# Layer 2 of a graph network: the last 72 of 196 steps of a strand gather a key and two projections in one row, and the picked projection is stored in edge order

## The chip, the cores and the metric

The kernel runs on one core of one Trainium2 chip. The metric is the device time of one execution in microseconds. A core has TensorE (matrix products, "PE"), VectorE ("DVE"), ScalarE ("ACT"), GpSimd ("POOL") and SyncE ("SP"); each runs its own instructions in order, and they wait for each other through semaphores. Plain DMAs are issued here by SP and ScalarE; the gathers, whose row numbers come from data, are issued by GpSimd. All share 16 DMA engines.

## The reference

Four graph layers run over 6250 nodes with 128 features and 100000 edges, each edge with a source, a target and one of 32 types. The change is in the third layer (layer 2):

```python
q = (x @ Wq_w + Wq_b)[dst]
k_base = (x @ Wk1)[src] + (h_rel @ Wk2)[edge_type] + Wk_b
score_base = jnp.sum(q * k_base, axis=-1)
scores = (score_base[:, None] + q @ v_rule.T) * scale
...                                   # softmax over edges of one target and one type, mean over 4 rules: attn_mean
proj = jnp.einsum('nd,rdo->nro', x, W_r)        # 32 projections of every node
msg = proj[src, edge_type] * attn_mean[:, None]
out = jax.ops.segment_sum(msg, dst, num_segments=n_nodes) + bias
```

So an edge needs two rows that hang on its source: the key x @ Wk1 of the source, for the score, and the projection of the source by the edge's type, for the message.

## The kernel before

Edges are sorted by target and lie in 128 partitions of 784; each partition's 784 edges are four strands of 196 steps (`STRANDS`, `STRIDE`). Nodes lie 50 to a partition (`NB`).

The score stage of layer 2 is `scores_and_projections` (names `l2s_...`). It goes through 98 turns of two steps, eight columns of 128 edges each. In each turn GpSimd issues eight gathers (line 2686), each fetching a 512-byte key for one edge per partition from `table_k` into one of six slots of `krow` (`KRING`). SP loads the rows with the queries, spread by target, into one of two slots of `zrow` (line 2695). VectorE carries the query along the strand, multiplies it with the keys and reduces (lines 2616 to 2631). GpSimd may fill a slot again when VectorE has used it. In 22 late turns one of the eight columns isn't gathered: TensorE picks it out of the keys in SBUF with one-hot matrices that VectorE and ScalarE write (`LatePicks`, lines 2515 to 2562).

Beside this, and independent of it, TensorE multiplies each of the 50 blocks of 128 nodes with the 32 weight matrices (line 2644). ScalarE copies the products into one of two halves of `proj` (line 2658) and stores it into the table `g.proj` in device memory (line 2662), 100 stores of 128 x 8 KB.

Then comes the sum of layer 2, `sum_strands` (names `l2z_...`), with the attention in front of it: VectorE makes the row numbers (lines 2384 and 2385), then the softmax (lines 2395 to 2461). Meanwhile GpSimd begins to gather the projections from `g.proj`, 784 gathers of 128 rows of 512 bytes (line 1104), 16 to a turn, into one of six slots (`RING`). In a turn VectorE weighs 16 columns (lines 1137, 1138) and then adds step by step over four strands (lines 1069, 1070); SP stores the running sums of each step in `g.prefix` (line 1113). The last turn of 16 is cut in two.

`tail2` (names `l2y_...`) begins by joining the four strands of each partition and the partitions among each other (`StrandCompletion`: four gathers at line 1300, a scan over 512 numbers, four scatters at line 1304); then GpSimd fetches the sum of every node (line 1376).

## Time and profile before

| what | us |
|---|---|
| three timed runs, median (lowest to highest) | 6673.84 (6673.53 to 6675.8) |
| the profiled execution | 6672.9 |
| its span in the trace | 6671.0 |

Shares of the span: VectorE 76%, GpSimd 69%, TensorE 50%, ScalarE 15%. The chain of waits that ended last covers only the last 1% of the span here, so it doesn't tell which stage is bound by what; the windows and the groups by line do. In the rows below, times are microseconds from the start of the span unless marked ns. A gather's row on GpSimd is the time in which it writes the transfer's descriptors, not the transfer. The queue q10 carries the DMAs that ScalarE issues, q1 those of SP and q0 those of GpSimd; a queue's share is the time of its packets, summed and divided by 16 engines and the window.

### The profile page before, as it was taken

The page shows a single profiled execution, that of the slowest core. Times are in us where ns is not written, and L with a number is a line of the kernel's source. Part 1 is how long each engine was busy: PE and PEld are TensorE (multiplying, and loading weights), DVE is VectorE, ACT ScalarE, POOL GpSimd, SP SyncE. Part 2 cuts the span into 40 slices and gives each one's busy share as a digit, 9 for nine tenths or more (in the row PEclk, how much of TensorE's full clock was granted, in tenths as well). Part 3 has the DMA queues.
Part 4 walks back from the last instruction along what each step waited for, and adds up shares of the span by engine and source line. Part 5 has one row for each costly group of instructions (what it writes and reads, how often), then busy time and mean ns, then how long its engine had stood idle before and what let it go on. Part 6 is the DMA issues. An engine that isn't in the chain of part 4 may idle for free. (4 is left out here: it accounts for less than half of the span.)

```text
span 6671.0 us, 61345 instructions
## 1 busy us (share of the span) xinstructions
PE 3327.2 (50%) x21638; PEld 2955.3 (44%) x21638; DVE 5039.4 (76%) x7174; ACT 998.4 (15%) x2297; POOL 4601.4 (69%) x4753
## 2 busy tenths in 40 slices
PE   7530117467777457777468847730000004777770
PEld 5530106367777457777443327730000003777770
DVE  8999998678898677787647779986443446888886
ACT  1013333200000010000034435520000003000002
POOL 0027777777777677777667777777777767777774
PEclk9999558789988778888789978865555556888885
DMA  3036020134444344444339974433343332333332
GB/s 60 1 149 255 2 36 13 26 86 115 114 115 115 99 115 109 110 110 110 99 131 345 354 264 126 122 87 107 103 109 103 104 91 59 112 112 112 112 112 71
DMA packets 588107, 763.09 MB, mean 114 GB/s; under 512 B 118267, under 2 KB 479585, under 8 KB 568345
## 3 DMA queue, kind: packets, MB, share of 16 engines
q1 hardware_dynamic: 416916, 375.57, 17.6%
q0 software_dynamic: 152672, 272.57, 17.2%
q10 hardware_dynamic: 18210, 111.02, 4.3%
q8 instruction: 171, 2.80, 0.2%
q14 instruction: 138, 1.13, 0.1%
HBM read 346.63 MB, written 412.16 MB: 114 GB/s over the span
## 5 line engine op out<-in xcount | busy, mean ns | idle before, releaser
L1104 POOL DMA_INDIRECT l2z_rows<-proj,l2z_idx x784 | 765.6, 977 | 246.1 <-issue 238.6
L2686 POOL DMA_INDIRECT l2s_krow<-table_k,l2s_idx x762 | 720.9, 946 | 232.3 <-issue 231.3
L1104 POOL DMA_INDIRECT l0z_rows<-table,l0z_idx x736 | 697.2, 947 | 234.7 <-issue 224.0
L928 POOL DMA_INDIRECT l3z_rows<-table,l3z_idx x736 | 694.4, 944 | 234.7 <-issue 224.0
L1104 POOL DMA_INDIRECT l1z_rows<-table,l1z_idx x736 | 694.5, 944 | 233.3 <-issue 214.0
L837 PE MATMUL l3z_pfound<-l3h_hn,l3h_hot 128*128 128x130 f32 x4800 | 642.4, 303 | 236.3 <-DVE l3h_hot L814 236.3
L837 PE MATMUL l1z_pfound<-g_x,l2o_xT 128*128 128x128 f32 x4800 | 638.3, 303 | 238.9 <-DVE l2o_xT L814 238.9
L837 PEld LDWEIGHTS l3z_pfound<-l3h_hn,l3h_hot 128*128 128x128 f32 x4800 | 634.5, 218 | 244.2 <-issue 237.2
L837 PEld LDWEIGHTS l1z_pfound<-g_x,l2o_xT 128*128 128x128 f32 x4800 | 630.5, 218 | 246.6 <-issue 239.0
L2098 POOL DMA_INDIRECT first_sj<-scores,first_atdst x504 | 525.8, 1043 | 169.5 <-issue 169.5
L837 PE MATMUL l0z_pfound<-first_rows,l0r_hot 128*128 128x140 f32 x3648 | 475.3, 294 | 91.5 <-DVE l0r_hot L814 91.5
L837 PEld LDWEIGHTS l0z_pfound<-first_rows,l0r_hot 128*128 128x128 f32 x3648 | 465.3, 200 | 102.1 <-DVE l0r_hot L814 102.1
L1137 DVE TENSOR_TENSOR l2z_msg<-l2z_rows,l2z_factors 128x1024 f32<-128x1024 f32 (+1 forms) x50 | 60.0, 1200 | 512.6 <-DMA l2z_rows<-proj,l2z_idx 512.2
L2644 PE MATMUL l2s_bank<-l2o_wr,l2o_xT 128*128 128x512 f32 x800 | 373.0, 622 | 93.8 <-ACT l2s_proj L2658 76.4
L814 DVE TENSOR_TENSOR l2o_xT<-l1z_pcode,l1z_pnames 128x3200 f32<-128x3200 f32 x96 | 330.2, 3481 | 21.8 <-PE l1z_pcode L823 21.7
L814 DVE TENSOR_TENSOR l3h_hot<-l3z_pcode,l3z_pnames 128x3200 f32<-128x3200 f32 x96 | 330.3, 3482 | 11.9 <-PE l3z_pcode L823 11.5
L607 POOL IOTA sd_nidi<- 128x50 int32 x1 | 0.2, 170 | 429.0 <-POOLq L60 429.0
L2542 PE MATMUL l2s_bank<-l2o_kn,l2o_xT 128*128 128x128 f32 x2200 | 291.4, 302 | 5.3 <-DVE l2o_xT L2523 5.3
L2542 PEld LDWEIGHTS l2s_bank<-l2o_kn,l2o_xT 128*128 128x128 f32 x2200 | 290.8, 219 | 5.4 <-issue 5.4
L2644 PEld LDWEIGHTS l2s_bank<-l2o_wr,l2o_xT 128*128 128x128 f32 x800 | 154.3, 198 | 312.2 <-issue 171.2
L900 DVE SCALAR_TENSOR_TENSOR l3z_acc<-l3z_acc,l3z_xx,l3z_msg 128x128 f32<-128x128 f32 x784 | 271.7, 347 | 25.9
L268 PE MATMUL sd_turn<-g_ident,prep_key 128*128 128x128 f32 x112 | 27.6, 428 | 487.3 <-DVE prep_key L245 481.8
(619 smaller groups left out, 7595.9 us busy)
## 6 DMA issues: line engine op xcount, KB each, us to landing
proj<-l2s_proj ACTq DMA_DIRECT2D x100, 1024.0 KB
spread_q<-prep_zero SPq DMA_DIRECT2D x98, 656.0 KB
l2s_zrow<-spread_q SPq DMA_DIRECT2D x98, 656.0 KB
prefix<-l0z_acc SPq DMA_DIRECT2D x196, 256.0 KB
prefix<-l2o_kn SPq DMA_DIRECT2D x196, 256.0 KB
prefix<-l2z_acc SPq DMA_DIRECT2D x196, 256.0 KB
prefix<-l3z_acc SPq DMA_DIRECT2D x48, 1040.0 KB
l2z_rows<-proj,l2z_idx POOLq DMA_INDIRECT x784
```

What stands on the lines that cost most here:

```text
L268: mm = self.nc.tensor.transpose(self.turn[q][:, u], self.keys[at % 2][:, c:c + P], self.g.ident[:])
L607: nc.gpsimd.iota(nid_i[:], pattern=[[1, NB]], base=EP, channel_multiplier=NB).then_inc(numbered, 1)
L814: self.nc.vector.tensor_tensor(self.hot[i][:, 0:hi - lo], bc_mid(self.code[:], hi - lo), bc_last(self.names[:, lo:hi], P), ALU.is_equal).t ...
L837: mm = self.nc.tensor.matmul(self.found[:], self.hot[i][:, b - lo], self.nodes[:, b], start=b == 0, stop=b == NB - 1)
L900: v.scalar_tensor_tensor(acc[:, c, u, 0:D], sum_before(k, u)[:, 0:D], w.factor(k, lo, u), msg[:, u], ALU.mult, ALU.add).then_inc(summed, 1)
L928: nc.gpsimd.indirect_dma_start(out=rows[:, k % RING, u, :], out_offset=None, in_=table, in_offset=bass.IndirectOffsetOnAxis(ap=idx[:, lo + ...
L1104: nc.gpsimd.indirect_dma_start(out=rows[:, k % RING, c * (hi - lo) + u, :], out_offset=None, in_=table, in_offset=bass.IndirectOffsetOnAxi ...
L1137: chain.add(self.v.tensor_tensor(msg[:, 0:half], rows[:, 0:half], bc_last3(factor[:, 0:half], D), ALU.mult))
L2098: nc.gpsimd.indirect_dma_start(out=sj[:, j, :], out_offset=None, in_=g.scores0, in_offset=bass.IndirectOffsetOnAxis(ap=at_dst[:, j:j + 1], ...
L2542: mm = self.nc.tensor.matmul(self.found, self.hot[:, b], self.nodes[:, b], start=b == 0, stop=b == NB - 1)
L2644: mm = nc.tensor.matmul(bank[m % 2][:, b], xT[:, i, :], wr[:, c:c + wide], start=True, stop=True)
L2686: nc.gpsimd.indirect_dma_start(out=krow[:, k % KRING, c * (hi - lo) + u, :], out_offset=None, in_=g.table_k, in_offset=bass.IndirectOffset ...
```

## The change

The last 72 of each strand's 196 steps ("late") are treated otherwise than the first 124 ("early").

- The projection table gets one and a half times as many rows: for each node and each pair of types three rows stand side by side, the even type's projection, the node's key, and the odd type's projection. ScalarE copies the key between them, one copy more per half block, and the 100 stores are 128 x 12 KB each.
- In the score stage the early part (62 turns) is as before, without `LatePicks`: all 496 keys are gathered. When all stores of the table have landed, GpSimd gathers in the late part (36 turns, 288 gathers) rows of 1536 bytes, key and two projections, into four places that lie over the room of `krow` and `proj`. VectorE uses the key in the middle. ScalarE scales the identity matrix by 1 or 0 for each column and parity; TensorE multiplies both projections with these and adds, so that the one of the edge's type is left; ScalarE copies it and stores it in edge order into `g.late`.
- The sum (`sum_halves`) treats the early and late steps as separate strands, eight in a partition, in turns of 16 columns: 31 early ones, gathered by GpSimd into four slots, and 18 late ones between them, loaded from `g.late` by SP in plain DMAs of 1 MB into two slots. Each part has one accumulator instead of two in turn. The last turn isn't cut.
- VectorE computes ends for eight half strands at the start of the score stage (`HalfEnds`), and the completion joins eight (`HalfCompletion`): eight gathers and scatters, a scan over 1024 numbers. The row numbers of the projections take six operations more.

```diff
+EARLY_STEPS, LATE_STEPS = 124, STRIDE - 124
+HALVES = 2 * STRANDS
+SLOTS = TYPES // 2 * 3
+EARLY, LATE = 4, 2
+PARTS = [(0, EARLY_STEPS), (EARLY_STEPS, STRIDE)]
+def both_parts():
+    n = [(hi - lo) // ABREAST for lo, hi in PARTS]
+    order = []
+    for i in range(n[0]):
+        order += [(1, m) for m in range(n[1] * i // n[0], n[1] * (i + 1) // n[0])] + [(0, i)]
+    return [(h, i, PARTS[h][0] + i * ABREAST, PARTS[h][0] + (i + 1) * ABREAST) for h, i in order]
...
+    def on_vector(self, chain):
+        v, g, keep, run, own = self.nc.vector, self.g, self.order.keep[:], self.run, self.base
+        lead = self.halves.full[:]
+        for s in range(HALVES):
+            lo, hi = (s // 2 * STRIDE + at for at in PARTS[s % 2])
+            chain.add(v.memset(run[:, lo:lo + 1], float(lo)))
+            chain.add(v.tensor_tensor_scan(run[:, lo + 1:hi], keep[:, lo + 1:hi], keep[:, lo + 1:hi], 1.0, ALU.mult, ALU.min))
+            chain.add(v.tensor_scalar(own[:, s:s + 1], g.part[:], float(HALVES), float(EP + 1 + s), ALU.mult, ALU.add))
...
+        chain(v.tensor_copy(self.halves.at_i[:], lead))
+        for h, (lo, hi) in enumerate(PARTS):
+            chain.add(v.tensor_reduce(self.halves.full[:, h::2], strands(keep, lo, hi), AX, ALU.min))
...
+class HalfCompletion:
...
+    def on_pool(self, pool):
+        where = self.halves.at_i
+        for s in range(HALVES):
+            self.nc.gpsimd.indirect_dma_start(out=self.row[:, s, :], out_offset=None, in_=self.prefix,
+                                              in_offset=bass.IndirectOffsetOnAxis(ap=where[:, s:s + 1], axis=0)).then_inc(self.lead, 16)
+        for s in range(HALVES):
+            pool.wait_ge(self.fixed, s + 1)
+            self.nc.gpsimd.indirect_dma_start(out=self.prefix, out_offset=bass.IndirectOffsetOnAxis(ap=where[:, s:s + 1], axis=0),
+                                              in_=self.row[:, s, :], in_offset=None).then_inc(self.sent, 16)
+        pool.wait_ge(self.sent, 16 * HALVES)
...
+        eng.wait_ge(self.turned, 1)
+        v.tensor_copy(self.tail[:], self.ps.rearrange("p (s q) -> p q s", s=HALVES)).then_inc(self.cleared, 1)
...
+        v.tensor_tensor_scan(shifted[:, 1:n], full[:, 0:n - 1], tail[:, 0:n - 1], 0.0, ALU.mult, ALU.add).then_inc(self.moved, 1)
+        eng.wait_ge(self.lead, 16 * HALVES)
+        eng.wait_ge(self.returned, 1)
+        for s in range(HALVES):
+            at = s // 2 * STRIDE + PARTS[s % 2][0]
+            v.scalar_tensor_tensor(self.row[:, s], self.back[:, s], self.order.keep[:, at:at + 1], self.row[:, s],
+                                   ALU.mult, ALU.add).then_inc(self.fixed, 1)
+def sum_halves(nc, name, g, order, table, late, prefix, halves, weight, aside):
+    with Space(nc, name) as s:
+        rows = s.sb("rows", [P, EARLY + LATE, WIDTH, D])
+        msg = s.sb("msg", [P, WIDTH, D])
+        acc = s.sb("acc", [P, 2, WIDTH, D])
...
+                for k, (h, i, lo, hi) in enumerate(turns):
+                    aside.on_vector(eng, chain, k)
+                    if k == 0:
+                        chain(v.tensor_copy(factors[:], by_step(weight)))
+                    if h:
+                        eng.wait_ge(got_late[i % LATE], 16 * (i // LATE + 1))
+                    else:
+                        eng.wait_ge(got_early[i % EARLY], 16 * n * (i // EARLY + 1))
+                    if i:
+                        eng.wait_ge(stored[h], 16 * ABREAST * i)
...
+                v.tensor_copy(g.tail[:], last[0])
+                v.tensor_copy(halves.tails[:], last[1])
...
+                for i, k in enumerate(early_turns):
+                    lo, hi = turns[k][2:]
+                    if i >= EARLY:
+                        hold(pool, weighed, early_turns[i - EARLY] + 1)
+                    for u in range(hi - lo):
+                        for c in range(STRANDS):
+                            nc.gpsimd.indirect_dma_start(out=rows[:, slot(i, 0), c * (hi - lo) + u, :], out_offset=None, in_=table,
+                                                         in_offset=bass.IndirectOffsetOnAxis(ap=idx[:, c, lo + u:lo + u + 1], axis=0)).then_inc(got_early[i % EARLY], 16)
...
+                def fetch(i):
+                    lo, hi = (at - EARLY_STEPS for at in turns[late_turns[i]][2:])
+                    sp.dma_start(rows[:, slot(i, 1), 0:STRANDS * (hi - lo)].rearrange("p (c u) f -> p c (u f)", c=STRANDS),
+                                 ready[:, :, lo * D:hi * D]).then_inc(got_late[i % LATE], 16)
+                for i in range(LATE):
+                    fetch(i)
+                done = 0
+                for k, (h, i, lo, hi) in enumerate(turns):
+                    for u in range(hi - lo):
+                        done += 1
+                        sp.wait_ge(summed, done)
+                        sp.dma_start(out[:, :, (lo + u) * D:(lo + u + 1) * D], by_strand(acc[:, h, 0:STRANDS * (hi - lo)])[:, :, u]).then_inc(stored[h], 16)
+                    if h and i + LATE < len(late_turns):
+                        sp.wait_ge(weighed, k + 1)
+                        fetch(i + LATE)
...
-        chain(v.scalar_tensor_tensor(self.most[:], g.src[:, 0:NC], float(TYPES), g.type[:], ALU.mult, ALU.add))
-        return v.tensor_copy(idx[:], self.most[:])
+        most, odd, bits = self.most, self.lead, self.trail[:].bitcast(I32)
+        chain(v.tensor_copy(bits, g.type[:]))
+        chain(v.tensor_scalar(bits, bits, 1, None, ALU.bitwise_and))
+        chain(v.tensor_copy(odd[:], bits))
+        chain(v.scalar_tensor_tensor(most[:], g.type[:], 3.0, odd[:], ALU.mult, ALU.add))
+        chain(v.tensor_scalar(most[:], most[:], 0.5, None, ALU.mult))
+        chain(v.scalar_tensor_tensor(most[:], g.src[:, 0:NC], float(SLOTS), most[:], ALU.mult, ALU.add))
+        return v.tensor_copy(idx[:], strands(most[:], 0, EARLY_STEPS))
...
-class LatePicks:
...
+        room = s.sb("room", [P, PLACES * n * place])
+        krow = room[:, 0:KRING * n * D].rearrange("p (r x f) -> p r x f", r=KRING, x=n)
+        proj = room[:, KRING * n * D:].rearrange("p (h j y f) -> p h j y f", h=2, j=TYPES // 4, y=3)
+        triple = room[:].rearrange("p (r x f) -> p r x f", r=PLACES, x=n)
...
-        late = range(54, len(turns), 2)
-        picks = LatePicks(nc, s, g, kn, xT, [(STRANDS - 1) * STRIDE + turns[k][1] - 1 for k in late], [bank[0][:, c, 0:P] for c in range(2)], bank[1][:, 0, 0:P])
...
-                picks.start(chain)
+                v.tensor_copy(strands(idx[:], 0, EARLY_STEPS), strands(g.src[:, 0:NC], 0, EARLY_STEPS)).then_inc(indexed, 1)
+                bits, odd, where = qv[:, 1].bitcast(I32), qv[:, 2], qv[:, 3]
...
+                ends.on_vector(chain)
...
+                    if m < 0:
+                        eng.wait_ge(got[k % KRING], 16 * n * (k // KRING + 1))
+                        keys = krow[:, k % KRING]
+                    else:
+                        eng.wait_ge(taken[at(m)], 16 * n * (m // PLACES + 1))
+                        keys = triple[:, at(m), :, D:2 * D]
+                    chain(v.tensor_tensor(prod[:, 0:n], keys, qrow[:, :, 0:D], ALU.mult))
...
-                picks.on_tensor(pe)
+                for m in range(len(turns) - early):
+                    pe.wait_ge(marked, m + 1)
+                    pe.wait_ge(taken[at(m)], 16 * n * (m // PLACES + 1))
+                    if m >= 2:
+                        pe.wait_ge(moved, m - 1)
+                    out = bank[m % 2][:].rearrange("p b (x f) -> p (b x) f", f=D)
+                    for x in range(n):
+                        for y in range(2):
+                            mm = nc.tensor.matmul(out[:, x], marks[:, m % 2, x, y], triple[:, at(m), x, 2 * y * D:(2 * y + 1) * D],
+                                                  start=y == 0, stop=y == 1)
+                    mm.then_inc(chosen, 1)
...
+                            c.copy(proj[:, h, :, 1], kn[:, i].unsqueeze(1).to_broadcast([P, TYPES // 4, D])).then_inc(between, 1)
...
+                        c.copy(proj[:, h, j:j + 4, 0::2], bank[m % 2][:].rearrange("p b (j y f) -> p (b j) y f", y=2, f=D)).then_inc(copied, 1)
...
+                            act.dma_start(table[:, i, h * SLOTS // 2 * D:(h + 1) * SLOTS // 2 * D],
+                                          proj[:, h].rearrange("p j y f -> p (j y f)")).then_inc(stored[h], 16)
...
+                def mark(m):
+                    if m >= 2:
+                        act.wait_ge(chosen, m - 1)
+                    for x in range(n):
+                        for y in range(2):
+                            made = c.activation(marks[:, m % 2, x, y], g.ident[:], ACT.Copy, scale=choice[:, y, x // 2, 2 * m + x % 2:2 * m + x % 2 + 1])
+                    made.then_inc(marked, 1)
+                last = len(turns) - early
+                mark(0)
+                for m in range(last):
+                    if m + 1 < last:
+                        mark(m + 1)
+                    act.wait_ge(chosen, m + 1)
+                    if m >= 2:
+                        act.wait_ge(sent[m % 2], 16 * (m // 2))
+                    c.copy(chosen_rows[:, m % 2], bank[m % 2][:].rearrange("p b (x f) -> p (b x) f", f=D)).then_inc(moved, 1)
+                    act.wait_ge(moved, m + 1)
+                    act.dma_start(ready[:, :, 2 * m * D:(2 * m + 2) * D],
+                                  chosen_rows[:, m % 2].rearrange("p (c u) f -> p c (u f)", c=STRANDS)).then_inc(sent[m % 2], 16)
...
+                pool.wait_ge(stored[0], 16 * NB)
+                pool.wait_ge(stored[1], 16 * NB)
+                both = g.proj.rearrange("(n r) f -> n (r f)", r=3)
+                for m, (lo, hi) in enumerate(turns[early:]):
+                    if m >= PLACES:
+                        pool.wait_ge(chosen, m - PLACES + 1)
+                        hold(pool, used, early + m - PLACES + 1)
+                    elif m >= 2:
+                        hold(pool, used, early)
+                    for u in range(hi - lo):
+                        for c in range(STRANDS):
+                            j = c * STRIDE + lo + u
+                            nc.gpsimd.indirect_dma_start(out=triple[:, at(m), c * (hi - lo) + u, :], out_offset=None, in_=both,
+                                                         in_offset=bass.IndirectOffsetOnAxis(ap=idx[:, j:j + 1], axis=0)).then_inc(taken[at(m)], 16)
...
-                sum_strands(nc, "l2z", g, O.dst, g.proj, g.prefix, D, Weighed(attn[:]), Beside(attention, tab3))
+                sum_halves(nc, "l2z", g, O.dst, g.proj, g.late, g.prefix, halves, attn[:], Beside(attention, tab3))
```

## Rows read from the trace of the kernel before

**Rows 1.** The page, costliest groups: line, operation, count | busy us, mean ns | idle before.

```profile
L1104 POOL DMA_INDIRECT l2z_rows<-proj,l2z_idx x784 | 765.6, 977 | 246.1 <-issue 238.6
```

**Rows 2.** Windows of GpSimd's gathers in the sum: window, length, busy (count), clock, DMA.

```profile
4445.20:4541.60 96.40, 79.24 (x57) 0.50 0.16 41
...
4541.60:5450.00 908.40, 686.37 (x728) 0.50 0.40 109
```

**Rows 3.** Window of all engines: PE, PEld, DVE, ACT, POOL, clock, DMA share, GB/s.

```profile
4540.00:5454.00 914.00, 0.58 (x2) 0.50 (x2) 385.27 (x493) 0.00 (x0) 687.67 (x729) 0.50 0.40 108
```

**Rows 4.** Gathers by tile: shortest/median/longest ns, first and last start (512-, 16-byte rows).

```profile
L2686 POOL DMA_INDIRECT l2s_krow<-table_k,l2s_idx x762: 940/944/1193, 3485.0 to 4436.9; - x191
...
L2098 POOL DMA_INDIRECT first_sj<-scores,first_atdst x504: 940/944/2149, 440.3 to 1206.6; - x168
```

**Rows 5.** Timeline of VectorE, the start of two following score turns.

```profile
4405.54 0.85 DVE L2616 TENSOR_TENSOR l2s_qrow<-l2s_qrow,g_dokeep 128x656 f32<-128x656 f32 x1
...
4413.68 0.85 DVE L2616 TENSOR_TENSOR l2s_qrow<-l2s_qrow,g_dokeep 128x656 f32<-128x656 f32 x1
```

**Rows 6.** Line 2662, the stores of the projections: issue ns, first and last issue.

```profile
L2662 ACTq DMA_DIRECT2D proj<-l2s_proj x100: 326/326/341, 3485.7 to 3932.5; - x100
```

**Rows 7.** Window of all engines over those stores, columns as in the third group.

```profile
3485.70:3937.00 451.30, 367.31 (x794) 151.95 (x792) 318.82 (x488) 199.90 (x212) 341.26 (x362) 0.96 0.95 351
```

**Rows 8.** DMA queues from 3500 to 3550 us: packets, MB, share of 16 engines.

```profile
q10 hardware_dynamic: 1460, 10.64, 51.1%
q1 hardware_dynamic: 2624, 3.34, 23.6%
q0 software_dynamic: 1280, 2.62, 17.8%
```

**Rows 9.** Groups by line, whole span: count | busy us, mean ns | idle before.

```profile
L2644 PE MATMUL l2s_bank<-l2o_wr,l2o_xT 128*128 128x512 f32 x800 | 373.0, 622 | 93.8 <-ACT l2s_proj L2658 76.4 <-PEq L60 14.7 <-issue 2.7
L2542 PE MATMUL l2s_bank<-l2o_kn,l2o_xT 128*128 128x128 f32 x2200 | 291.4, 302 | 5.3 <-DVE l2o_xT L2523 5.3
L2658 ACT COPY l2s_proj<-l2s_bank 128x1024 f32<-128x1024 f32 x200 | 198.3, 1013 | 268.9 <-DMA proj<-l2s_proj 145.4 <-PE l2s_bank L2644 123.2
L2555 ACT ACTIVATE l2o_xT<-l2s_bank,l2s_pnames 128x128 f32<-128x128 f32 x572 | 151.8, 401 | 234.6 <-PE l2s_bank L2542 233.7 <-PE l2s_bank L2528 0.9
```

**Rows 10.** DMA issues: count, KB each, median us from issue to landing.

```profile
table_q<-l1y_qn SPq DMA_DIRECT2D x12, 328.0 KB, 2.8
```

**Rows 11.** DMA queues from 4800 to 4850 us (512-byte rows out, projections in).

```profile
q0 software_dynamic: 1287, 2.65, 21.7%
q1 hardware_dynamic: 5280, 2.62, 17.9%
```

**Rows 12.** DMA queues from 1000 to 1050 us, gathers of 16-byte rows.

```profile
q0 software_dynamic: 1062, 0.07, 5.3%
```

**Rows 13.** Timeline of the attention and of a turn of the sum.

```profile
4468.29 4.17 POOL L1104 DMA_INDIRECT l2z_rows<-proj,l2z_idx  x1 [0.30 <-issue]
...
4539.05 1.22 DVE L1137 TENSOR_TENSOR l2z_msg<-l2z_rows,l2z_factors 128x1024 f32<-128x1024 f32 x1
...
4547.40 1.22 DVE L1137 TENSOR_TENSOR l2z_msg<-l2z_rows,l2z_factors 128x1024 f32<-128x1024 f32 x1
```

**Rows 14.** Timeline of the ends of both stages and of the completion.

```profile
4436.86 0.95 POOL L2686 DMA_INDIRECT l2s_krow<-table_k,l2s_idx  x1 [0.30 <-issue]
...
4443.45 0.97 DVE L2384 SCALAR_TENSOR_TENSOR l_attn<-g_src,g_type 128x784 f32<-128x784 f32 x1 [1.13 <-PEq L60]
...
5448.60 0.95 POOL L1104 DMA_INDIRECT l2z_rows<-proj,l2z_idx  x1 [0.31 <-issue]
...
5451.07 0.69 DVE L1137 TENSOR_TENSOR l2z_msg<-l2z_rows,l2z_factors 128x512 f32<-128x512 f32 x1 [5.20 <-DMA l2z_rows<-proj,l2z_idx]
...
5460.85 0.94 POOL L1300 DMA_INDIRECT l2y_leadrow<-prefix,g_dostrandi  x1 [11.30 <-POOLq L60]
...
5474.07 0.98 POOL L1376 DMA_INDIRECT l2y_agg<-prefix,g_doendi  x1 [1.54 <-DMA prefix<-l2y_leadrow,g_dostrandi]
```

More of the change, by code:

```diff
@@ new lines, with __init__ @@
+class HalfEnds:
+    def __init__(self, nc, g, order, halves, run, base):
+        self.nc, self.g, self.order, self.halves, self.run, self.base = nc, g, order, halves, run, base
+    def on_vector(self, chain):
[6 more added lines that the diff above has]
+            chain.add(v.tensor_scalar(own[:, s:s + 1], g.part[:], float(HALVES), float(EP + 1 + s), ALU.mult, ALU.add))
+        chain.until()
+        for h, (lo, hi) in enumerate(PARTS):
+            chain.add(v.tensor_reduce(lead[:, h::2], strands(run, lo, hi), AX, ALU.add))
+        chain.until()
+        chain(v.scalar_tensor_tensor(lead, g.part[:].to_broadcast([P, HALVES]), float(NC), lead, ALU.mult, ALU.add))
+        chain(v.tensor_tensor(lead, lead, own, ALU.subtract))
+        for h, (lo, hi) in enumerate(PARTS):
+            chain.add(v.tensor_tensor(lead[:, h::2], lead[:, h::2], strands(keep, lo, lo + 1)[:, :, 0], ALU.mult))
+        chain.until()
+        chain(v.tensor_tensor(lead, lead, own, ALU.add))
+        chain(v.tensor_copy(self.halves.at_i[:], lead))
+        for h, (lo, hi) in enumerate(PARTS):
+            chain.add(v.tensor_reduce(self.halves.full[:, h::2], strands(keep, lo, hi), AX, ALU.min))
+        chain.until()
@@ L1732, in tail2 @@
         xT = s.sb("xT", [P, 2, GROUP, P])
-        tp, ph = s.ps("tp", [P, GROUP, P]), [s.ps(f"ph{u}", [P, W3]) for u in range(GROUP)]
-        done = StrandCompletion(nc, s, g, O.dst, g.prefix, tp[:], s.ps("cpb", [P, STRANDS, P])[:])
+        turns_ps, ph = s.ps("tp", [P, HALVES * P]), [s.ps(f"ph{u}", [P, W3]) for u in range(GROUP)]
+        tp = turns_ps[:, 0:GROUP * P].rearrange("p (u q) -> p u q", u=GROUP)
+        done = HalfCompletion(nc, s, g, O.dst, halves, g.prefix, turns_ps[:], s.ps("cpb", [P, HALVES, P])[:])
         inner, outer = Norm(nc, s, g, "a"), Norm(nc, s, g, "b")
@@ L2586, in scores_and_projections, with at @@
         stepped, used = s.sem("stepped"), s.sem("used")
-        multiplied, copied = s.sem("multiplied"), s.sem("copied")
+        multiplied, copied, between = s.sem("multiplied"), s.sem("copied"), s.sem("between")
+        marked, chosen, moved = s.sem("marked"), s.sem("chosen"), s.sem("moved")
         stored = [s.sem(f"stored{h}") for h in range(2)]
-        late = range(54, len(turns), 2)
-        picks = LatePicks(nc, s, g, kn, xT, [(STRANDS - 1) * STRIDE + turns[k][1] - 1 for k in late], [bank[0][:, c, 0:P] for c in range(2)], bank[1][:, 0, 0:P])
-        def landed(k):
-            return 16 * sum(n - (m in late) for m in range(k % KRING, k + 1, KRING))
+        sent = [s.sem(f"sent{h}") for h in range(2)]
         got, zgot = [s.sem(f"got{r}") for r in range(KRING)], [s.sem(f"zgot{h}") for h in range(2)]
+        taken = [s.sem(f"taken{r}") for r in range(PLACES)]
+        ends = HalfEnds(nc, g, order, halves, qv[:, 0], own[:])
+        def at(m):
+            return (m + 2) % PLACES
         with s.block() as block:
@@ L2649, in _ @@
             @block.scalar
             def _(act):
[L2651 removed]
+                c = nc.scalar
+                table = g.proj.rearrange("(p b r) f -> p b (r f)", b=NB, r=SLOTS)
                 for i in range(NB):
                     for k in range(pairs):
[L2654 to L2656 removed]
+                        m, h, j = i * pairs + k, k // 2, k % 2 * 4
+                        if k % 2 == 0:
+                            if i:
+                                act.wait_ge(stored[h], 16 * i)
+                            c.copy(proj[:, h, :, 1], kn[:, i].unsqueeze(1).to_broadcast([P, TYPES // 4, D])).then_inc(between, 1)
@@ L2657, in _ @@
                         act.wait_ge(multiplied, m + 1)
-                        nc.scalar.copy(proj[:, c], bank[m % 2][:].rearrange("p b f -> p (b f)")).then_inc(copied, 1)
+                        c.copy(proj[:, h, j:j + 4, 0::2], bank[m % 2][:].rearrange("p b (j y f) -> p (b j) y f", y=2, f=D)).then_inc(copied, 1)
                         if k % 2:
                             act.wait_ge(copied, m + 1)
-                            c = slice(2 * (k - 1) * wide, 2 * (k + 1) * wide)
-                            act.dma_start(table[:, i, c], proj[:, c]).then_inc(stored[h], 16)
@@ L2663, in _ @@
-                picks.squares(act, 0)
-                for m, k in enumerate(late):
-                    picks.squares(act, m + 1)
-                    act.wait_ge(used, k - KRING + 1)
-                    picks.place(act, m, krow[:, k % KRING, n - 1])
+                            act.wait_ge(between, 2 * i + h + 1)
+                            act.dma_start(table[:, i, h * SLOTS // 2 * D:(h + 1) * SLOTS // 2 * D],
+                                          proj[:, h].rearrange("p j y f -> p (j y f)")).then_inc(stored[h], 16)
@@ L2677, in _ @@
                 pool.wait_ge(indexed, 1)
-                for k, (lo, hi) in enumerate(turns):
+                for k in range(early):
+                    lo, hi = turns[k]
                     if k >= KRING:
```

196 lines of the change are left out of this document (120 added, 76 removed).

## The prediction

> **What bounds the kernel now.** I read the costliest groups of the page first: at their head stand the 784 gathers that GpSimd issues in the sum of layer 2 [rows 1]; the windows then say how densely. In the sum, after its attention, 728 gathers fill 908.4 us, so one is issued every 908.4/728 = 1.248 us [rows 2]; there VectorE is busy 385 of 914 us and the DMA engines 0.40 of the time, at a granted TensorE clock of 0.50 with PE idle [rows 3]. In the score stage the first and the last of 762 gathers start 951.9 us apart, 1.251 us each [rows 4]. A VectorE turn there takes 8.14 us with its wait in it [rows 5], eight gathers 9.98 us. So both stages last as long as GpSimd needs to issue their gathers; what takes a gather away from GpSimd takes 1.248 us from the kernel, until something else is late. The exception is a stretch at the start of the score stage: from 3485.7 to 3937 us the DMA engines are 0.95 busy while the projections are stored [rows 6, 7]; GpSimd is not slowed by it yet, because nothing in that stage waits for the stores.
>
> All sums are made against the profiled execution, 6672.9 us; the median of the timed runs is 6673.84, 0.9 us more, which is below what I can resolve.
>
> **Part 1: gathers removed and added.** The sum gathers 31 turns x 16 = 496 rows instead of 784: 288 x 1.248 = **-359.4 us**. All 288 lie behind the attention, where no VectorE work stretches them: in the attention's 96.4 us only 57 gathers are issued [rows 2], and the new ring of four slots of 16 has room for 64, so the smaller ring costs nothing there. The score stage gathers 784 again instead of 762 (the 22 rows that TensorE picked are gone): 22 x 1.25 = **+27.5 us**. The one-hot work that goes with those picks (VectorE, ScalarE, TensorE) was beside GpSimd's issue and gives nothing back.
>
> Is a gather of 1536 bytes a row issued as fast as one of 512? The trace has none. Gathers of 16-byte rows take 944 ns (median), gathers of 512-byte rows 944 ns [rows 4]: no dependence on bytes over a factor of 32. I take 1.248 us; the other bound, three times that price, is the last rival.
>
> **Part 2: GpSimd now waits for the projection stores.** The first wide gather may start only when all 100 stores have landed. They grow from 104.9 MB (100 x 128 x 8 KB) to 157.3 MB. Before, the stores ran from 3485.7 us until about 3937 [rows 6]: 104.9/451 = 0.2325 MB/us. The upper bound on that rate comes from the queues' shares: keys and spread rows take 17.8% + 23.6%, leaving 58.5%, and the store queue moves 10.64 MB in 50 us at 51.1%, or 0.416 MB/us alone [rows 8]; 0.585 x 0.416 = 0.243 MB/us. GpSimd's early part is 496 x 1.2485 = 619 us, from 3485 to 4104, plus 3 us for the longer VectorE start (below): 4107. By then 144 MB are stored (150 at the upper rate); 13 MB remain (7). With the other two queues silent the rate rises, limited by two buffers: filling one takes three copies of about 1.01 us [rows 9] and the issue, 3.4 us, landing 2.8 (a store of 328 KB [rows 10]), moving 1.57 MB at 0.416 3.8 us; half of 10.0 is 5.0 us for 1.57 MB, 0.315 MB/us. 13/0.315 = **+41 us** of wait; between 15 (upper rate, all through) and 60 (a rate of 0.223). What hides the third copy per buffer is that ScalarE waits for landed stores 145 us in this stage [rows 9]. TensorE needs 373/50 = 7.5 us of a block's 13 us [rows 9].
>
> **Part 3: what the 36 late turns contain.** A turn is 8 wide gathers, 9.98 us of GpSimd. Beside it: VectorE 7.4 to 8.1 us as before [rows 5]. TensorE: 16 products, two instructions each, at 291.4/2200 = 0.132 us [rows 9], 4.2 us; twice that, 8.5, at the clock of 0.50 that [rows 3] shows. ScalarE: 16 scaled identities at 151.8/572 = 0.265 (throughput) to 0.401 us (one alone) [rows 9], 4.2 to 6.4 us, a copy of 1.01 and an issue: 5.6 to 7.8 us. Marks and banks are double-buffered, so these run side by side; each is below 9.98. DMA time per engine: 32 packets of spread rows at 0.236 x 800 us/2624 = 72 ns, 2.3 us [rows 8]; 32 kilobyte packets of the store between 46 and 54 ns (a 512-byte one takes 27.1 ns [rows 11]), 1.5 to 1.7 us; 64 wide rows. A 512-byte row of the projection table takes 0.217 x 800/1287/4 = 33.7 ns, a 16-byte row 0.053 x 800/1062/4 = 10 ns [rows 11, 12]; the line through both gives 82 ns for 1536 bytes, the bounds are 59 (at the store queue's 0.416 MB/us) and 101 (three times 33.7): 3.8 to 6.5 us. Sum 9.1 us, between 7.6 and 10.5, against 9.98. That is close. I take **0** for excess, because the mid value fits and a share of 0.95 was reached in [rows 7]; the upper end, 10.5/0.95 = 11.05, would cost 36 x 1.07 = +38.
>
> **Part 4: edges.** (a) Score stage's start: some 35 small VectorE operations more, about 14 us by their sizes. VectorE then starts 7 us later, which six turns of ring hide, but it slows GpSimd's issue: in the attention's 96.4 us, 57 gathers went out where 77 fit [rows 2], a quarter lost; of 14 us **+3** (0 to 5). The Trainium skill, page "SBUF — State Buffer", section "Who interferes with whom", says that a VectorE instruction with two SBUF inputs or in a two-port mode shuts GpSimd out for its whole length; by it only the new scans and two-input operations would count, an estimate of 3 us or less. The trace agrees in the one place where they meet: a gather takes 4.17 us beside such an operation [rows 13]. (b) Score stage's end: from the last gather's end (4437.8) to the next stage's first work (4443.45) were 5.7 us [rows 14]. Now the last turn goes landing 1.5 [rows 14], TensorE 4.2 to 8.5, copy 1.0, issue 0.4, landing of the store 2.8 [rows 10], block end 1: about 14.5, **+9** (5 to 14). (c) Indices: six more VectorE operations before GpSimd may start, **+3.2**. (d) The sum's last turn is 16 rows instead of 8, with 8.35 us of VectorE [rows 13] instead of some 4, and a second copy of tails: **+4.5**. (e) The completion joins 8 half strands instead of 4: four gathers and four scatters more in the 13.2 us from 5460.85 to 5474.07 [rows 14], 8 x 1.27 = 10.2; its longer chain of transposes and copies lies beside the lead gathers: **+10.5** (6 to 15).
>
> (f) VectorE in the sum: 49 turns x 8.35 = 409 us plus 99 for the attention, and 12 places where two early turns follow each other and the second waits some 3 us for the first one's stores: 545 us after the stage's start. GpSimd ends at 5 + 96 + 439 x 1.248 = 649. So GpSimd stays the bound with 100 us to spare. SP now also issues 18 loads of 1 MB in order among its stores; a slot has three turns until it is needed.
>
> **Sum.** -359.4 + 27.5 + 41 + 3 + 9 + 3.2 + 4.5 + 10.5 = -260.7; 6672.9 - 260.7 = **6412 us**. With the low ends of the bounds (wait 15, start 0, tail 5, completion 6) 6374; with the high ends but no excess of the late turns 6442; with it 6480.
>
> **Rivals.** (1) *Transfers bound the late turns*: 11.05 us a turn, 6412 + 38 = 6450. For it: 9.1 of 9.98 is near the limit, and three queues meet. Against: the shares of [rows 8] leave room, and the rings hold four turns. The Trainium skill, page "DMA: Bandwidth & Descriptors", section "Measured", gives 0.95 us for a transfer of 64 KB and 6.15 for 1 MB; a line between them makes 1.6 us for 192 KB, an estimate of 13.1 us a turn and 6526 us. The row says otherwise: a 64 KB gather takes 0.217 x 50/41 = 0.26 us of the engines' time [rows 11], since neighbours overlap, so that figure is no end of my range.
>
> (2) *Picking is serial*: marks, products and copy of one turn follow each other, 6.4 + 8.5 + 1.3 = 16.2 us a turn, 36 x 6.2 = +224: 6636. For it: ScalarE does both marks and copies in one order. Against: marks of the next turn are issued before the wait for this turn's products.
>
> (3) *VectorE becomes the sum's bound*: with one accumulator per part, every turn waits for a store behind a 1 MB load, 8.35 + 5.8 us x 49 + 99 = 792 instead of 649: +143, 6555. Against: the parts alternate in 36 of 48 steps.
>
> (4) *Slower than before*: GpSimd's price of a wide gather grows with its bytes. Place: the issue of the 288 late gathers. At three times 1.248 it is +719: 7131. It decides from 261/288 = 0.91 us more a gather, an issue every 2.16 us. Against it: 944 ns at 16 and at 512 bytes [rows 4]; for it only that no row is wider than 656 bytes.
>
> **How the numbers follow.** Forecast 0.72, rival 1 0.12, rival 2 0.07, rival 3 0.04, rival 4 0.05. The range 6374 to 6480 takes in the forecast's bounds and rival 1; rivals 2 to 4 (0.16) and a little of the rest are outside. Everything but rival 4 is faster: 0.94 faster, 0.05 slower, 0.01 within 0.2%, which is about what a measurement of this kernel can tell from no change.
>
> **What would show it.** The sum's gathers 1.248 us apart and the stage some 650 us to its last one; a gap of GpSimd near 4107 us that ends with the last projection store near 4148; the late gathers about 944 ns each and 9.98 us a turn. Rival 1 shows as GpSimd waiting in the late turns with a DMA share over 0.95; rival 2 as VectorE done and GpSimd waiting for TensorE; rival 3 as VectorE waiting for prefix stores; rival 4 as longer gathers. A gap much over 60 us would make part 2 wrong, a turn over 11 us part 3.

## The result, and the profile after

The changed kernel takes **6370.4 us** (median; 6368.2 to 6373.4), the kernel before 6673.7: a ratio of 0.9545 [0.9529, 0.9562]. The profiled execution took 6371.9, its span 6370.0, 301.0 less than before. The forecast was 6412 with a range from 6374: right in direction, 42 us too slow, and 3.6 us outside at the low end.

The gathers by tile (operation, count: shortest/median/longest ns, first and last start) answer to [rows 4]; below them is what GpSimd waited for ahead of its wide gathers (us, times):

```profile
L2896 POOL DMA_INDIRECT l2s_room<-table_k,l2s_idx x496: 940/944/1194, 3485.6 to 4105.7; - x166
L2911 POOL DMA_INDIRECT l2s_room<-proj,l2s_idx x288: 942/946/1164, 4106.9 to 4466.5; - x144
...
  issue: 85.9, 282
  DVE l_base L2809: 1.8, 6
```

A wide gather (line 2911) is issued in 946 ns, a key gather in 944. GpSimd lost 1.8 us to VectorE in the late turns, nothing to TensorE, and nothing to the stores. GpSimd's timeline at the four seams of layer 2, with what ended its wait in brackets:

```profile
4105.70 0.94 POOL L2896 DMA_INDIRECT l2s_room<-table_k,l2s_idx  x1 [0.30 <-issue]
4106.95 0.95 POOL L2911 DMA_INDIRECT l2s_room<-proj,l2s_idx  x1 [0.30 <-issue]
...
4466.54 0.94 POOL L2911 DMA_INDIRECT l2s_room<-proj,l2s_idx  x1 [0.30 <-issue]
4488.48 0.94 POOL L1304 DMA_INDIRECT l2z_rows<-proj,l2z_idx  x1 [20.99 <-DVE l2z_idx L2606]
...
5131.90 0.94 POOL L1304 DMA_INDIRECT l2z_rows<-proj,l2z_idx  x1 [0.30 <-issue]
...
5172.76 0.98 POOL L1590 DMA_INDIRECT l2y_agg<-prefix,g_doendi  x1 [1.53 <-DMA prefix<-l2y_leadrow,l_ati]
```

Between the last key gather and the first wide one lie the usual 0.30 us: the wait for the stores, put at 41 us, is not there. The stores (line 2853, answering to [rows 6]) show why:

```profile
L2853 ACTq DMA_DIRECT2D proj<-l2s_room x100: 326/326/350, 3485.8 to 4069.1; - x100
```

The last was issued at 4069.1. In the three runs below in which GpSimd does wait for it, the wait ends 5.9 to 8.5 us after that issue; so all had landed by about 4077 here, some 30 us before GpSimd asked. The forecast had them end near 4148.

The windows of the late turns and of the sum (PE, PEld, DVE, ACT, POOL busy, clock, DMA share, GB/s) answer to [rows 3, 7], the group of the sum's gathers to [rows 1]:

```profile
4146.00:4466.00 320.00, 158.55 (x1024) 153.38 (x1024) 228.71 (x351) 184.74 (x545) 242.33 (x256) 0.75 0.86 275
...
4488.00:5132.00 644.00, 6.84 (x27) 4.09 (x27) 470.62 (x549) 3.43 (x4) 492.69 (x496) 0.50 0.54 156
```

```profile
L1304 POOL DMA_INDIRECT l2z_rows<-proj,l2z_idx x496 | 493.5, 995 | 171.8 <-issue 148.7
```

In late turns no engine is full and the DMA engines are 0.86 busy: GpSimd's issue still sets the pace, as it does in the sum. Where the 301 us came from, by first and last gathers:

| stretch | before | after | difference | forecast |
|---|---|---|---|---|
| start of the span to the first key gather | 3485.0 | 3485.6 | +0.6 | +3 |
| first to last gather of the score stage | 951.9 | 980.9 | +29.0 | +27.5 and 41 of wait |
| on to the first gather of the sum | 8.4 | 21.9 | +13.5 | +12.2 |
| first to last gather of the sum | 1003.3 | 643.4 | -359.9 | -359.4 |
| on to the first gather of node sums | 25.5 | 40.9 | +15.4 | +15.0 |

The five differences add up to -301.4, the span fell by 301.0. Every term but one fits within 3 us, and the sum without the wait, 6412 - 41 = 6371, is the profiled time to 1 us. That last agreement is partly luck: the other terms are off by -2.4, +1.5, +1.3, -0.5 and +0.4, which cancel.

### The profile page after: what moved, and what is told of

Same layout as the page of the kernel before. It is cut to its first block and busy times, and to the rows that moved or that the text cites. A ratio compares the mean times of both kernels' runs of the same rounds, so it can differ in the third digit from the quotient of the medians.

```text
span 6370.0 us, 58942 instructions
## 1 busy us (share of the span) xinstructions
PE 3257.2 (51%) x20526; PEld 2848.6 (45%) x20526; DVE 4990.7 (78%) x7203; ACT 1071.1 (17%) x2371; POOL 4365.4 (69%) x4495
## 5 line engine op out<-in xcount | busy, mean ns | idle before, releaser
L1304 POOL DMA_INDIRECT l2z_rows<-proj,l2z_idx x496 | 493.5, 995 | 171.8 <-issue 148.7
L2896 POOL DMA_INDIRECT l2s_room<-table_k,l2s_idx x496 | 470.2, 948 | 151.1 <-issue 151.1
L2822 PE MATMUL l2s_bank<-l2o_wr,l2o_xT 128*128 128x512 f32 x800 | 417.6, 675 | 184.8 <-ACT l2s_room L2849 170.1
L2911 POOL DMA_INDIRECT l2s_room<-proj,l2s_idx x288 | 273.1, 948 | 87.7 <-issue 85.9
L2806 DVE TENSOR_TENSOR l2s_prod<-l2s_room,l2s_qrow 128x1024 f32<-128x1024 f32 x98 | 119.5, 1220 | 254.4 <-DMA l2s_room<-table_k,l2s_idx 160.3
L2833 PE MATMUL l2s_bank<-l2s_room,l2o_xT 128*128 128x128 f32 x1152 | 184.1, 335 | 226.3 <-issue 153.2
L2833 PEld LDWEIGHTS l2s_bank<-l2s_room,l2o_xT 128*128 128x128 f32 x1152 | 178.3, 248 | 232.7 <-issue 216.2
```

The lines of the kernel that those rows point to most:

```text
L1304: nc.gpsimd.indirect_dma_start(out=rows[:, slot(i, 0), c * (hi - lo) + u, :], out_offset=None, in_=table, in_offset=bass.IndirectOffsetOnA ...
L2806: chain(v.tensor_tensor(prod[:, 0:n], keys, qrow[:, :, 0:D], ALU.mult))
L2822: mm = nc.tensor.matmul(bank[m % 2][:, b], xT[:, i, :], wr[:, c:c + wide], start=True, stop=True)
L2833: mm = nc.tensor.matmul(out[:, x], marks[:, m % 2, x, y], triple[:, at(m), x, 2 * y * D:(2 * y + 1) * D], start=y == 0, stop=y == 1)
L2896: nc.gpsimd.indirect_dma_start(out=krow[:, k % KRING, c * (hi - lo) + u, :], out_offset=None, in_=g.table_k, in_offset=bass.IndirectOffset ...
L2911: nc.gpsimd.indirect_dma_start(out=triple[:, at(m), c * (hi - lo) + u, :], out_offset=None, in_=both, in_offset=bass.IndirectOffsetOnAxis( ...
```

## Why the stores were early: the queues

The DMA queues over 400 us in the thick of the stores (packets, MB, share of 16 engines; q10 the stores, q1 the spread rows, q0 the gathers). Before:

```profile
q10 hardware_dynamic: 12620, 91.85, 56.5%
q1 hardware_dynamic: 20644, 26.27, 21.3%
q0 software_dynamic: 10236, 20.99, 16.9%
```

After:

```profile
q10 hardware_dynamic: 9628, 105.14, 63.7%
q1 hardware_dynamic: 21073, 26.81, 20.7%
q0 software_dynamic: 10224, 20.95, 15.2%
```

The forecast left 58.5% for the stores, since the other two queues held 41.4% [rows 8]. They did not hold it. For the same bytes (47.3 and 47.8 MB) they show 38.2% over these 400 us before and 35.9% after, and the stores take 63.7%. The store queue moved 0.263 MB/us instead of 0.230. What differs is how often ScalarE had nothing to send: with a buffer free it waited 96.6 us for products before, and 16.5 us after. Its waits over the same 400 us (us in total, times, longest), before and then after:

```profile
ACT l2s_proj L2658 <- DMA proj<-l2s_proj: 131.2, 46, 5.5
ACT l2s_proj L2658 <- PE l2s_bank L2644: 96.6, 91, 3.0
```

```profile
ACT l2s_room L2847 <- DMA proj<-l2s_room: 188.2, 67, 5.5
ACT l2s_room L2849 <- PE l2s_bank L2822: 16.5, 18, 2.0
```

Before, ScalarE waited in turn for a buffer and for TensorE, which itself waits for ScalarE's copies [rows 9]; while one half is filled, only the other can be on its way. With stores of 1.5 times the bytes that gap comes once per 1.57 MB instead of 1.05, and the products are ready when a buffer is. That is **theory A**: the rate of before was set by its two buffers, not by the engines. **Theory B**: longer rows (12 KB instead of 8) move at a better price. The forecast's own reading was a third: the other queues' shares are a fixed price and the engines were as good as full.

## Experiments

**Before, with three store buffers of 8 KB instead of two.** The bytes and row lengths are those of before, so B and the fixed shares expect no change of the store rate.

```diff
-        proj = s.sb("proj", [P, TYPES * D])
+        proj = s.sb("proj", [P, 3, 4 * wide])
...
-        stored = [s.sem(f"stored{h}") for h in range(2)]
+        stored = [s.sem(f"stored{h}") for h in range(3)]
...
+                        h = at % 3
+                        if at >= 3 and k % 2 == 0:
+                            act.wait_ge(stored[h], 16 * (at // 3))
```

> The kernel before with three store buffers of 8 KB a partition in place of two, nothing else. Theory A (before the change the store queue ran dry between stores, because a buffer was filled only after its last store had landed): the stores keep the queue full, move 0.26 to 0.27 MB/us as after the change, the last is issued near 3875 us in place of 3932.5, the DMA share of the stretch rises from 0.95 to about 1.0. Theory B (rows of 12 KB are cheaper per byte than rows of 8 KB): the rate stays near 0.233 MB/us and the last store is issued between 3920 and 3935. Time by both: 6674 us, no change, since nothing waits for the stores.

The time did not move: 6673.7 against 6673.6, ratio 1.000 [0.9989, 1.0010]; nobody waits for these stores. But they were issued until 3845.4 instead of 3932.5 [rows 6]. First the line of the stores, then the queues from 3500 to 3840 us:

```profile
L2663 ACTq DMA_DIRECT2D proj<-l2s_proj x100: 325/326/341, 3488.1 to 3845.4; - x100
```

```profile
q10 hardware_dynamic: 13541, 98.61, 69.2%
q1 hardware_dynamic: 17409, 22.15, 18.6%
q0 software_dynamic: 8674, 17.79, 13.9%
```

The stores moved 98.61/340 = 0.290 MB/us, a fifth over the "upper bound" of 0.243; the small queues fell to 32.5% at an unchanged 0.117 MB/us (39.94/340; before 47.26/400 = 0.118). Theory A holds in direction, and a queue's share is no fixed price. Its figures were too low: it expected 0.26 to 0.27 MB/us and a last issue near 3875, because it took the queue of the change as full. The change's two buffers leave gaps too. [rows 7] with its 351 GB/s and share of 0.95 was a queue that ran dry, not a limit.

TensorE's clock is another rival: a faster TensorE would leave shorter gaps as well. The windows of the kernel before, of the change (both 3500 to 3900 us) and of the three buffers (3500 to 3840) show busy times, granted clock, DMA share and GB/s:

```profile
3500.00:3900.00 400.00, 326.53 (x700) 135.32 (x701) 289.17 (x443) 174.40 (x176) 302.50 (x320) 0.96 0.95 348
...
3500.00:3900.00 400.00, 280.84 (x536) 110.49 (x536) 288.15 (x440) 195.10 (x202) 302.66 (x320) 0.90 1.00 383
...
3500.00:3840.00 340.00, 329.38 (x754) 140.09 (x752) 244.06 (x372) 188.29 (x189) 257.40 (x272) 1.00 1.02 408
```

The change stores faster than the kernel before at a lower mean clock, 0.90 against 0.96, so the clock isn't the reason there. With three buffers it is 1.00, the higher of its two levels (2.4 GHz) throughout, where the other means mix it with the lower one; TensorE waited only 10.0 us for ScalarE's copies there, before 71.0 in its 400 us. But 4% more clock doesn't make 26% more stores. Each rate comes from one profile, and rates vary: in the run without picked keys below, which leaves the store loop as it is, two 8 KB buffers moved 86.60 MB in the same 400 us, 0.217 MB/us, at a clock of 0.91. That is 6% less than before; the differences read here are 14% and 26%.

**The change, each store sent as two of 6 KB rows**, same buffers: theory B expects a slower rate, theory A the same.

```diff
-                                act.wait_ge(stored[h], 16 * i)
+                                act.wait_ge(stored[h], 32 * i)
...
-                            act.dma_start(table[:, i, h * SLOTS // 2 * D:(h + 1) * SLOTS // 2 * D],
-                                          proj[:, h].rearrange("p j y f -> p (j y f)")).then_inc(stored[h], 16)
+                            for part in range(2):
+                                lo, size = h * SLOTS // 2 * D + part * SLOTS // 4 * D, SLOTS // 4 * D
+                                act.dma_start(table[:, i, lo:lo + size],
+                                              proj[:, h, 4 * part:4 * part + 4].rearrange("p j y f -> p (j y f)")).then_inc(stored[h], 16)
```

> The changed kernel with each store of 128 x 12 KB issued as two DMAs of 128 x 6 KB, one behind the other, same bytes and same waits. Theory A (queue kept full): the last store is issued within 10 us of 4069 and the time stays at 6370 us. Theory B (long rows): at 6 KB the keys' and spread rows' queues take 38% again and the store queue 0.406 MB/us of its share, so 0.251 MB/us; stores end near 4112, GpSimd waits 5 to 10 us, 6375 to 6382 us.

6366.9 us (6365.7 to 6372.7), ratio 0.9542 [0.9527, 0.9558]: that of the change. Its store queue from 3500 to 3900 us:

```profile
q10 hardware_dynamic: 19169, 104.70, 64.8%
```

That is 104.70 MB against 105.14 in the change, with twice the packets, or 0.262 MB/us where theory B expected 0.251; the last store was issued at 4077.0, 8 us later than in the change. So the row length is not what changed the rate, and theory B is refuted.

**Before, without the picked keys**: all 784 gathered, the +27.5 us alone.

```diff
-        late = range(54, len(turns), 2)
-        picks = LatePicks(nc, s, g, kn, xT, [(STRANDS - 1) * STRIDE + turns[k][1] - 1 for k in late], [bank[0][:, c, 0:P] for c in range(2)], bank[1][:, 0, 0:P])
+        late = []
...
-                picks.start(chain)
...
-                picks.on_tensor(pe)
```

> The kernel before without the 22 late columns picked by TensorE: 784 keys gathered, no one-hot work in the score stage. Theory (GpSimd's issue sets the stage): 22 x 1.25 = +27.5 us, 6699 to 6703 us. Rival (the one-hot work also sits on the path, so that its removal gives something back): +10 to +20 us.

6696.8 us (6696.3 to 6701.0): ratio 1.0037 [1.0023, 1.0051], +23.2 us. The gathers by tile:

```profile
L2682 POOL DMA_INDIRECT l2s_krow<-table_k,l2s_idx x784: 940/944/1177, 3482.0 to 4461.3; - x196
```

From first to last 979.3 us, +27.4 over [rows 4]: the term is right. The time itself, +23.2, lies between the theory's 26 to 30 and the rival's 10 to 20, and its interval (+15 to +34) reaches into both; the trace decides. The stage begins 3.0 us earlier in this profile, but that comes from ahead of it: the first gather of layer 0's sum starts at 1361.4 us already, against 1363.7 before, where both kernels are the same. From the stage's first VectorE instruction to its first key gather it is 5.7 us in both (3476.33 to 3482.03, 3479.26 to 3484.97), so the removal of the picks gives nothing back.

In the changed kernel it is 6.3 us (3479.28 to 3485.57): the four gathers ahead of the first key gather took 4.42 us instead of 3.84, and that is the +0.6 of the table, where +3 had been forecast.

**Where the wait begins.** If the stores end at 4077 and GpSimd asks at 3486 + 4.99 x (steps of the early part), the wait is zero at 124 and appears near 118; each step moved from the early to the late part saves four gathers in the sum, 5.0 us, until then, and nothing after. One line is changed, with 132, 120, 116 and 108:

```diff
-EARLY_STEPS, LATE_STEPS = 124, STRIDE - 124
+EARLY_STEPS, LATE_STEPS = 116, STRIDE - 116
```

> The changed kernel with 132 early and 64 late steps. Theory (GpSimd's issue sets both stages, the stores are ready before GpSimd asks): 32 gathers more in the sum, 32 x 1.248 = +40 us: 6410 us (6406 to 6414). No wait for stores.

> 120 early and 76 late steps. Stores land near 4080 us, GpSimd ends its early part at 3485.6 + 480 x 1.25 = 4086: no wait, 16 gathers fewer in the sum, -20 us: 6350 us (6347 to 6354). Rival (two more late turns cost more than 9.98 us each, by the DMA engines): 6354 to 6362.

> 116 early and 80 late steps. GpSimd ends its early part at 4066 and waits until the stores have landed, about 4078: 12 us; -40 + 12 = -28: 6342 us (6336 to 6350).

> 108 early and 88 late steps. GpSimd's early part ends at 4026. By then 143 MB are stored; 14 MB remain and move at 0.315 to 0.34 MB/us once the key gathers are silent: stores land near 4071, wait about 45 us; -80 + 45 = -35: 6335 us (6325 to 6350). Rival (the stores are no faster alone, 0.265 MB/us): landed at 4080, wait 54: 6344 us.

| early steps | us (lowest to highest) | ratio to before | GpSimd asks | wait for the stores |
|---|---|---|---|---|
| 132 | 6419.7 (6417.4 to 6420.3) | 0.9605 [0.9589, 0.9621] | 4151.8 | 0 |
| 124, the change | 6370.4 (6368.2 to 6373.4) | 0.9545 [0.9529, 0.9562] | 4106.9 | 0 |
| 120 | 6355.5 (6352.2 to 6358.4) | 0.9511 [0.9495, 0.9527] | 4087.4 | 0 |
| 116 | 6349.1 (6347.8 to 6349.5) | 0.9500 [0.9484, 0.9516] | 4067.0 | 19.9 |
| 108 | 6341.8 (6339.0 to 6343.6) | 0.9490 [0.9474, 0.9506] | 4031.9 | 38.6 |

These four stood beside a kernel before of 6682.6 us, 9 more than beside the change, so the change is compared with them by the ratio. GpSimd's timeline at the seam with 120, 116 and 108:

```profile
4086.11 0.94 POOL L2896 DMA_INDIRECT l2s_room<-table_k,l2s_idx  x1 [0.30 <-issue]
4087.35 0.95 POOL L2911 DMA_INDIRECT l2s_room<-proj,l2s_idx  x1 [0.30 <-issue]
```

```profile
4066.03 0.94 POOL L2896 DMA_INDIRECT l2s_room<-table_k,l2s_idx  x1 [0.30 <-issue]
4086.85 0.94 POOL L2911 DMA_INDIRECT l2s_room<-proj,l2s_idx  x1 [19.87 <-DMA proj<-l2s_room]
```

```profile
4030.99 0.95 POOL L2896 DMA_INDIRECT l2s_room<-table_k,l2s_idx  x1 [0.30 <-issue]
4070.57 0.94 POOL L2911 DMA_INDIRECT l2s_room<-proj,l2s_idx  x1 [38.63 <-DMA proj<-l2s_room]
```

So the mechanism of Part 2 exists and looks as it was described, a gap of GpSimd that ends with a store; its place is between 120 and 116 steps and not at 124. From 132 to 120 twelve steps gave 64.2 us (48 x 1.248 = 59.9 by gathers); from 120 to 108 twelve more gave 13.8. Carried over by the ratio to the 6673.7 us of the result, the four are 6410, 6347, 6340 and 6333 us, where 6410, 6350, 6342 and 6335 were expected; the medians as they stand put 132 and 120 outside their ranges. The waits were expected at 0, 0, 12 and 45 us. The ratio's interval of 10 us to each side doesn't exclude the rival for 120 (6354 to 6362), but in its trace the wide gathers go out 1.257 us apart, against 1.253 in the change.

**Four slots instead of two halves, in the same room.** By A more, smaller stores in the air should end sooner; then a smaller early part pays again. A slot is 6 KB a partition, stored as soon as its four pairs are copied.

```diff
-        proj = room[:, KRING * n * D:].rearrange("p (h j y f) -> p h j y f", h=2, j=TYPES // 4, y=3)
+        proj = room[:, KRING * n * D:].rearrange("p (h j y f) -> p h j y f", h=4, j=TYPES // 8, y=3)
...
+                        if i:
+                            act.wait_ge(stored[k], 16 * i)
+                        c.copy(proj[:, k, :, 1], kn[:, i].unsqueeze(1).to_broadcast([P, TYPES // 8, D])).then_inc(between, 1)
...
+                        act.dma_start(table[:, i, k * SLOTS // 4 * D:(k + 1) * SLOTS // 4 * D],
+                                      proj[:, k].rearrange("p j y f -> p (j y f)")).then_inc(stored[k], 16)
```

> The changed kernel with the store buffer's room cut into four slots of 128 x 6 KB in place of two of 12 KB: a slot is filled while up to three stores are under way, 200 stores in place of 100. Theory A (what limits the stores is that the queue runs dry between a landing and the next fill): 0.28 MB/us or more in place of 0.265, the last store lands before 4050 us in place of about 4080; the time stays at 6370 us, since GpSimd asks at 4107. Rival (the DMA engines are full in either case): landing at 4075 to 4085.

> Four slots and 112 early, 84 late steps. GpSimd's early part ends at 3486 + 448 x 1.25 = 4046. Theory A: wait of 0 to 6 us, 48 gathers fewer in the sum, -60: 6313 us (6308 to 6322). Rival (stores no faster than with two buffers): wait of 30, 6340 us.

> Four slots and 104 early, 92 late steps. GpSimd's early part ends at 4006, stores land about 4041: wait 35; 80 gathers fewer in the sum, -100 + 35 = -65: 6308 us (6300 to 6320). So past the point where the two meet, fewer early steps bring next to nothing.

With 124 steps 6369.6 us (6367.4 to 6373.9), ratio 0.9542 [0.9526, 0.9558]: no gain, as nothing waits. Its stores by line, and its queue from 3500 to 3900 us:

```profile
L2851 ACTq DMA_DIRECT2D proj<-l2s_room x200: 325/326/392, 3487.4 to 4034.2; - x100
```

```profile
q10 hardware_dynamic: 20866, 113.96, 69.7%
q1 hardware_dynamic: 20577, 26.18, 18.5%
q0 software_dynamic: 10238, 20.99, 14.1%
```

The last issue is 35 us earlier, the rate 113.96/400 = 0.285 MB/us (0.28 or more was expected), the queue's share that of the three buffers. With 112 steps it takes 6310.3 us (6310.2 to 6312.7), 0.9454 [0.9438, 0.9470], without a wait, and with 104 **6301.3** (6298.7 to 6302.2), 0.9440 [0.9424, 0.9455]: the best version of this study, 69 us under the change. At 104 the wait is back, 29.3 us where 35 were expected: from 112 to 104 the sum has 32 gathers fewer, 40 us, and 9.0 came out. A still shorter early part was not run; by this it would lengthen the wait by most of what it saves. GpSimd's timeline there:

```profile
4009.04 0.94 POOL L2895 DMA_INDIRECT l2s_room<-table_k,l2s_idx  x1 [0.30 <-issue]
4039.27 0.95 POOL L2910 DMA_INDIRECT l2s_room<-proj,l2s_idx  x1 [29.29 <-DMA proj<-l2s_room]
```

## Why the prediction was right, and where wrong

**What failed** is one term of Part 2: +41 us of GpSimd waiting for the stores, and its low bound of 15. It took 0.2325 MB/us as the going rate, and 58.5% of the engines times 0.416 MB/us as the most the store queue could have. Both figures were read off a state in which the queue was short of work. GpSimd waited 0 us, since the stores went at 157.3/592 = 0.266 MB/us. Scaling the time of a store by its bytes made it 1.5 x 4.51 = 6.8 us; it took 592/100 = 5.9 (from the first key gather to the last landing). The 0.416 was sound: 105.14 MB in 400 us at 63.7% make 0.413. Wrong was to take the rest of the engines' time for spoken for, from a window of 50 us at the stage's very start, where the store queue shows 51.1% [rows 8] while over 400 us it shows 56.5%. The rows that should have warned stood in the prediction itself: ScalarE waiting 145 us for stores and 123 us for TensorE [rows 9], beside a queue that is "full", means too few buffers. The low bound doesn't follow from the prediction's own sum either: at 0.243 MB/us all through, 157.3 MB end at 4133, a wait of 26 us and not of 15. A low bound without any wait would have made the range reach 6359.

**What held.** Part 1: 288 gathers fewer are -359.4 as worked out, -359.9 as measured; the smaller ring cost next to nothing, as GpSimd waited 2.1 us in all for one of its slots. The 22 picked gathers are +27.4 by an experiment. A row of 1536 bytes is issued like one of 512: 946 and 944 ns, so rival 4 is refuted. Part 3: 10.02 us a turn for 9.98. The engines' time of a wide row is 77 ns against a forecast of 82, from this row of 4200 to 4250 us: 7.54 MB are 4909 rows of 1536 bytes, and 47.2% of 16 engines' 50 us, 378 us, divided by them:

```profile
q0 software_dynamic: 2446, 7.54, 47.2%
```

A turn has 0.86 x 10.02 = 8.6 us of DMA time where 9.1 was forecast, so rival 1 did not come. The Trainium skill, page "DMA: Bandwidth & Descriptors", section "Measured", from which 1.6 us for 192 KB had been worked out, is not borne out as a spacing of gathers: 288 of them went out 1.25 us apart with the engines 0.86 busy.

Rival 2: GpSimd never waited for TensorE. The last turn shows how the picking runs, all engines:

```profile
4471.10 6.25 PE L2833 MATMUL l2s_bank<-l2s_room,l2o_xT 128*128 128x128 f32 x32 [6.25 <-issue]
...
4477.38 1.01 ACT L2874 COPY l2o_wr<-l2s_bank 128x1024 f32<-128x1024 f32 x1 [11.48 <-PE l2s_bank L2833]
4478.42 0.52 ACTq L2876 DMA_DIRECT2D late<-l2o_wr  x1
...
4483.35 0.57 DVE L2600 CAST l2b_trail<-g_type 128x784 int32<-128x784 f32 x1 [9.32 <-PEq L60]
```

6.25 us lies within the 4.2 to 8.5 of Part 4 (b). From the last gather's end (4467.5) to the next stage's first work (4483.35) it is 15.9 us, 10.2 more than before, for +9; the row numbers then take 5.1 us instead of 1.9, for +3.2 (they take five operations more, not six). Rival 3: VectorE waited ahead of its turns for gathers, hardly for the stores of sums (us, times):

```profile
  DMA l2z_rows<-proj,l2z_idx: 136.8, 21
  DMA prefix<-l2z_acc: 15.1, 4
```

The edges came to +0.6 (for +3), +13.5 (for 12.2) and +15.4 (for 15.0).

## What to carry to other kernels

A busy share of 0.95 over a stretch is no ceiling as long as an engine that feeds a queue waits for buffers in it: look at the feeder's waits and at the longest window before a rate is scaled, and give such a term a low end at which the wait is zero. Where a new wait is priced, find the point at which it starts (here: steps of the early part), since one line moved by a few steps says on which side one stands. More slots of smaller stores in the same room can be worth more than larger stores, once somebody waits for the last of them.

## What the runs showed of the hardware

The same small transfers (0.118 MB/us on two queues) took 38.2% of the engines' time beside stores of 0.230 MB/us, 35.9% beside 0.263 and 32.5% beside 0.290; with three buffers the shares add up to 102%, so packets overlap in these records. Why the small packets' time falls was not settled. Throughput went from 348 to 408 GB/s. The Trainium skill, page "HBM Reference", section "Specifications (TRN2)", says that a core streaming alone gets well above its share of 358 GB/s, up to some 425; the 408 agrees.

Whether VectorE stretches a gather depends on where its two inputs lie. The completion's scan has both in SBUF, the memory in which the row numbers of a gather lie as well; here it is with the gather beside it:

```profile
5153.57 2.29 DVE L1214 TENSOR_TENSOR_SCAN l2y_shifted<-l2y_allfull,l2y_alltail 128x1023 f32<-128x1023 f32 x1
...
5153.75 2.87 POOL L1181 DMA_INDIRECT l2y_leadrow<-prefix,l_ati  x1 [0.30 <-issue]
```

In the score stage a product left its gather at 0.94 us:

```profile
4413.43 1.22 DVE L2806 TENSOR_TENSOR l2s_prod<-l2s_room,l2s_qrow 128x1024 f32<-128x1024 f32 x1 [6.33 <-DMA l2s_room<-proj,l2s_idx]
4414.02 0.94 POOL L2911 DMA_INDIRECT l2s_room<-proj,l2s_idx  x1 [0.30 <-issue]
```

Of this product's inputs only `l2s_room` lies in SBUF; `l2s_qrow` lies in PSUM, the other memory on the core (`s.ps` in the kernel). A product with both inputs in SBUF does stretch its gather. In the kernel before, the gather of 4.17 us at 4468.29 [rows 13] starts beside this one:

```profile
4468.21 3.42 DVE L2429 TENSOR_TENSOR l2b_bwd<-l_qv,l_attn 128x3136 f32<-128x3136 f32 x1
```

The prediction had taken from the Trainium skill's page "SBUF — State Buffer", section "Who interferes with whom", that a VectorE instruction with two SBUF inputs holds up GpSimd; by these rows that is so for the scan and for the product alike, and not for the product with one input in PSUM.
